# Layer 3 attention of a four-layer decoder: score blocks in cycles of three instead of two

## The reference

```python
def _L3_attn_ref(x, proj_w, proj_b, wq, wk):
    ...
    proj = jnp.einsum('bsd,ed->bse', x, proj_w) + proj_b
    flat = jnp.transpose(proj.reshape(B, S, H, hd), (2, 0, 1, 3)).reshape(H, B * S, hd)
    q = jnp.einsum('hnd,hde->hne', flat, wq)
    k = jnp.einsum('hnd,hde->hne', flat, wk)
    logits = jnp.einsum('hne,hme->hnm', q, k) / jnp.sqrt(jnp.asarray(D, x.dtype))
    attn = jax.nn.softmax(logits, axis=-1)
    out = jnp.einsum('hnm,hmd->hnd', attn, flat)
    ...
x = x + _L3_attn_ref(_layernorm(x, axis=-1), L3_attn_proj_w, L3_attn_proj_b, L3_attn_wq, L3_attn_wk)
```

## Time and profile before

| | us |
|---|---|
| median of 3 runs | 3333.8 (3326.77 to 3339.62) |
| span of the profiled execution | 3397.0 |
| probes and scores run, in that span | 2430 to 3142 |
| PE busy, whole span | 3009.1 (89%) |
| DVE busy | 2235.3 (66%) |
| ACT busy | 1822.0 (54%) |
| POOL busy | 1132.7 (33%) |

### The profile page before, as it was taken

One profiled execution on the slowest core, in us unless ns is written; L12 is line 12 of the kernel. 1 busy time (PEld: TensorE's weight loads), 2 busy tenths in 40 slices (PEclk: granted clock), 3 DMA queues, 4 the chain that ended last, 5 costly groups with the idle time before them and its releaser, 6 DMA issues. The chain is left out here.

```text
span 3397.0 us, 59298 instructions
## 1 busy us (share of the span) xinstructions
PE 3009.1 (89%) x20925; PEld 1857.6 (55%) x20929; DVE 2235.3 (66%) x4489; ACT 1822.0 (54%) x4182; POOL 1132.7 (33%) x1288
## 2 busy tenths in 40 slices
PE   7979759998887799987799989797799999999889
PEld 4656548877664556653467657454333333333567
DVE  6777645454546656667567747525589999996672
ACT  6967713333213344445566645211278888888554
POOL 3535555433432022215166653012111111221333
PEclk9999869999998999998889999898789999999989
DMA  9300156665530000022000032132401111110300
GB/s 301 133 9 2 47 203 210 207 188 173 158 101 26 26 1 1 1 73 85 33 1 1 1 118 106 64 109 88 113 1 20 20 21 20 21 20 1 125 13 25
DMA packets 158228, 243.61 MB, mean 72 GB/s; under 512 B 21298, under 2 KB 130482, under 8 KB 152482
## 3 DMA queue, kind: packets, MB, share of 16 engines
q1 hardware_dynamic: 144114, 202.05, 19.6%
q0 software_dynamic: 13824, 37.77, 3.4%
HBM read 132.64 MB, written 107.10 MB: 71 GB/s over the span
## 5 line engine op out<-in xcount | busy, mean ns | idle before, releaser
L4783 DVE TENSOR_REDUCE peaks<-ps 128x2 f32<-128x1024 f32 x512 | 617.6, 1219 | 64.8 <-PE ps L4727 63.0
L4820 ACT ACTIVATE attn<-ps 128x512 f32<-128x512 f32 x1024 | 558.8, 596 | 113.1 <-PE ps L4717 56.8
L4717 PE MATMUL ps<-queries,keys 50*128 50x512 f32 x1024 | 383.8, 455 | 0.0
L4727 PE MATMUL ps<-keys,queries 50*128 50x512 f32 x1024 | 370.2, 468 | 12.8 <-DVE peaks L4783 7.9
L4742 PE MATMUL ps<-attn,head_values 128*32 128x256 f32 x4096 | 332.3, 397 | 9.2 <-ACT output L4831 9.2
L4717 PEld LDWEIGHTS ps<-queries,keys 50*128 50x128 f32 x1024 | 157.6, 188 | 215.6 <-ACT attn L4820 197.5
L1239 POOL TENSOR_TENSOR attn_w<-attn_w,attn_share 128x512 f32<-128x512 f32 x128 | 131.7, 1050 | 373.0 <-DVE attn_share L1085 373.0
L2133 PE MATMUL ps<-experts,tileT 128*128 x884 | 232.0, 385 | 2.1 <-issue 2.1
L2340 DVE COPY normed<-ps 128x256 f32<-128x256 f32 x221 | 93.8, 424 | 202.9 <-PE ps L2149 106.8
L4742 PEld LDWEIGHTS ps<-attn,head_values 128*32 128x32 f32 x4096 | 82.3, 108 | 197.9 <-issue 108.6
L2194 ACT ACTIVATE tileT<-ps 128x256 f32<-128x256 f32 x221 | 84.6, 383 | 168.4 <-PE ps L2117 115.7
(11 more groups left out here) (733 smaller groups left out, 7164.5 us busy)
## 6 DMA issues: line engine op xcount, KB each, us to landing
tile_in<-routed_rows SPq DMA_DIRECT2D x244, 128.0 KB, 2.2
expert_rows<-normed SPq DMA_DIRECT2D x221, 128.0 KB
routed_rows<-zeros SPq DMA_DIRECT2D x2, 8064.0 KB, 48.1
experts<-in_L_ffn_experts SPq DMA_DIRECT2D x4, 3072.0 KB
routed_rows<-zeros SPq DMA_DIRECT2D x1, 12160.0 KB, 67.0
kT<-L_xattn_keys SPq DMA_DIRECT2D x8, 1024.0 KB
v<-L_xattn_values SPq DMA_DIRECT2D x8, 1024.0 KB, 8.7
experts<-in_L_ffn_experts SPq DMA_DIRECT2D x8, 1024.0 KB
```

What stands on the lines that cost most here:

```text
L4717: nc.tensor.matmul(bank(("score", n)), keys[pair % 2][rows, sl(kt)], queries[pair % 2][rows, sl(c, CHUNK)], start=True, stop=True).then_in ...
L4727: last = nc.tensor.matmul(k.ps[:, SB + p % PB, :], queries[pair % 2][rows, sl(t)], keys[pair % 2][rows, sl(c, CHUNK)], start=True, stop=True)
L4783: v.tensor_reduce(peaks[:, r % 2, i // CHUNKS, :, i % CHUNKS], k.ps[:, at:at + 2, :], AX.X, ALU.max).then_inc(s["maxed"], 1)
L4820: nc.scalar.activation(attn[:, n % RING, :], bank(("score", n)), ACT.Exp, scale=1.0 / 16.0).then_inc(s["read"], 1)
```

## The change

The loop on PE goes in cycles of three score blocks. With n0 the first of the three, a cycle does: probe n0 + 49, score n0, score n0 + 1, probe n0 + 50, probe n0 + 51, score n0 + 2 (one probe, number 0, is done ahead of the loop). These six alternate between the halves of the array. Then come, as a rule, three quarters of a mixing, 128 columns each: a unit has 32 quarters, spread over its 10 or 11 cycles, with 2 to 4 in a cycle. A call of `mix` takes the quarters of one mixing, so a cycle that passes from one mixing to the next has two calls. `unturn` stands at the end of a cycle, `out` and `take` on ACT follow the same cycles, and the places of POOL's and DVE's small steps move by 2 or 3 blocks (`SUM` from 17 to 20, `DIVIDE` from 24 to 26). The banks (4 for probes, 3 for scores) and the ring of 16 stay as they were, and so does every instruction of DVE's reductions and ACT's exponentials.

```diff
+        CYCLE, QUARTER, MIX_BEHIND = 3, CHUNK // 4, 8
         steps = range(-LEAD, TOTAL + SPAN)
-        OUT, UNTURN, SUM, DIVIDE, TURN, RAISE = 6, 15, 17, 24, 5, 8
+        UNTURN, SUM, DIVIDE, TURN, RAISE = 15, 20, 26, 5, 8
...
+        quarters_in, ended_in = {}, {}
+        for u_ in range(UNITS):
+            at = u_ * SPAN + MIX_BEHIND
+            cycles = range(at + -at % CYCLE, at + SPAN, CYCLE)
+            for i, n_ in enumerate(cycles):
+                quarters_in[n_] = range(u_ * SPAN + i * SPAN // len(cycles), u_ * SPAN + (i + 1) * SPAN // len(cycles))
+            ended_in[cycles[-1]] = u_
...
-                def mix(m, half):
+                def mix(m, first, last_one):
                     u, part = m // 8, m % 8
-                    columns = sl(half, CHUNK // 2)
+                    columns = slice(first * QUARTER, (last_one + 1) * QUARTER)
...
-                for n in steps:
-                    if n < 16 - LEAD and n % 4 == 0:
-                        value(4 + (n + LEAD) // 4)
-                    if n % 2 == 0:
-                        for p in (n + LEAD, n + LEAD + 1):
-                            if p < TOTAL:
-                                probe(p)
-                        if scored(n):
+                probe(0)
+                for n0 in steps[::CYCLE]:
+                    for n in range(n0, n0 + CYCLE):
+                        if n < 16 - LEAD and n % 4 == 0:
+                            value(4 + (n + LEAD) // 4)
+                    for n in range(n0, n0 + CYCLE):
+                        p = n + LEAD + 1
+                        if n == n0 + 1 and scored(n):
                             score(n)
-                        if scored(4 * (n // 4 - 2)):
-                            mix(n // 4 - 2, n % 4 // 2)
-                        if scored(n + 1):
-                            score(n + 1)
-                    if ended_at(n, UNTURN) is not None:
-                        unturn(ended_at(n, UNTURN))
+                        if p < TOTAL:
+                            probe(p)
+                        if n != n0 + 1 and scored(n):
+                            score(n)
+                    quarters = quarters_in.get(n0, ())
+                    for m in sorted({q // 4 for q in quarters}):
+                        here = [q % 4 for q in quarters if q // 4 == m]
+                        mix(m, here[0], here[-1])
+                    if unturned_at(n0 + CYCLE - 1) is not None:
+                        unturn(unturned_at(n0 + CYCLE - 1))
...
-                    if ended_at(n, OUT) is not None:
-                        out(ended_at(n, OUT))
-                    if ended_at(n, UNTURN) is not None:
-                        take(ended_at(n, UNTURN))
+                    if n - CYCLE + 1 in ended_in:
+                        out(ended_in[n - CYCLE + 1])
+                    if unturned_at(n) is not None:
+                        take(unturned_at(n))
```

More of the change, by code:

```diff
@@ L4647, in l3_attn @@
         mixed_bank = k.ps[:, 7, :]
+        CYCLE, QUARTER, MIX_BEHIND = 3, CHUNK // 4, 8
         steps = range(-LEAD, TOTAL + SPAN)
-        OUT, UNTURN, SUM, DIVIDE, TURN, RAISE = 6, 15, 17, 24, 5, 8
+        assert LEAD % CYCLE == 0 and len(steps) % CYCLE == 0
+        UNTURN, SUM, DIVIDE, TURN, RAISE = 15, 20, 26, 5, 8
         def scored(n):
@@ L4660, in ended_at, with unturned_at @@
             return u if n % SPAN == i and 0 <= u < UNITS else None
+        def unturned_at(n):
+            found = [ended_at(n - i, UNTURN) for i in range(CYCLE)] if n % CYCLE == CYCLE - 1 else []
+            return next((u for u in found if u is not None), None)
+        quarters_in, ended_in = {}, {}
[5 more added lines that the diff above has]
+            ended_in[cycles[-1]] = u_
         slot_of = {}
@@ L4664, in l3_attn @@
             jobs = [("score", n_)] if scored(n_) else []
-            if ended_at(n_, UNTURN) is not None:
-                jobs.append(("unturn", ended_at(n_, UNTURN)))
+            if unturned_at(n_) is not None:
+                jobs.append(("unturn", unturned_at(n_)))
             for job in jobs:
@@ L4730, in probe @@
                         last.then_inc(s["probed"], 1)
-                def mix(m, half):
+                def mix(m, first, last_one):
                     u, part = m // 8, m % 8
-                    columns = sl(half, CHUNK // 2)
-                    if half == 0:
+                    columns = slice(first * QUARTER, (last_one + 1) * QUARTER)
+                    if first == 0:
                         pe.wait_ge(s["read"], slot_of["score", 4 * m + 3] + 1)
-                    if part == 0 and half == 0:
+                    if part == 0 and first == 0:
                         pe.wait_ge(s["fetched"], u // CHUNKS + 1)
@@ L4742, in mix @@
                         last = nc.tensor.matmul(mixed_bank[sl(strip, PAD), columns], head_values[:, u // CHUNKS % 2, strip % 2, 2 * part + strip // 2, :],
-                                                attn[:, (4 * m + strip) % RING, columns], start=part == 0 and half == 0, stop=part == 7 and half == 1,
-                                                skip_group_check=True)
-                    if half == 1:
+                                                attn[:, (4 * m + strip) % RING, columns], start=part == 0 and first == 0,
+                                                stop=part == 7 and last_one == 3, skip_group_check=True)
+                    if last_one == 3:
                         last.then_inc(s["mixed"], 1)
```

## The result

The changed kernel takes 3388.6 us (median of 4 runs, 3382.3 to 3397.6), the one before, run beside it, 3336.3 us (3326.8 to 3339.6). The ratio is 1.0171, with a 95% interval from 1.0148 to 1.0194: 52 us slower. Forecast were 3382 us and 48 us slower.

What follows compares the result with a forecast made beforehand. PE was taken as the bound before, a PE-DVE loop through the probe banks after. 29.6 units at 1.6 us more (49 unrounded), less 2 at the low clock, added 48 to 3333.8: 3382 us, range 3345 to 3425.

Steps and rivals of the forecast that it cites:

- PE set the pace before: Runs and half mixings on PE take 1.233 us per two score blocks; DVE's reductions follow at 1.13.
- PE's work falls to 1.67 a cycle: Run of six 0.89 plus mixing 0.78 gives 1.67 us for three blocks, where 1.85 were.
- The loop: Waiting probe, mixing, partner probe and reductions: 3.02 + 1.13 = 4.15 us for three pairs, 1.385 a pair against 1.233.
- What a unit has once: Transposes add 0.35 us and DVE's small steps 0.23 to the loop's share; a unit takes 22.7 us, 1.6 more.
- The copy to `output`: The mixing's wait for `outed`, 0.36 us per unit, goes, since the next mixing comes a whole run of 0.89 later.
- The number of units and the low clock: 474 pairs are 29.6 units, 49 us more unrounded; 14 pairs at the low clock save 2 us.
- second calls of `mix`: Four added weight loads in half of the cycles, up to 0.03 us each time, +5 us at most, taken as nothing.
- probes alone, DVE's pace in both: First 24 pairs of the stage run at DVE's pace before and after, so no difference was counted.
- Signs named ahead: Reduction spacing 1.13, 1.13, 1.9; DVE idle 100 to 140 us; PE's probe waits 80 to 130; unit 22.4 to 23.2.
- Rival 1: Probe wait costs nothing and shorter PE work pays out: unit about 19.1 us, kernel 3275 us; chance 0.10.
- Rival 2: Clock falls as the loop leaves PE idle about 0.8 us of every 4.15: some 3480 us; chance 0.06.
- Rival 3: Waiting PE pulls probe weight loads ahead, 0.22 off the loop: unit 21.5 us, kernel 3345 us; chance 0.04.

Runs made afterwards that it cites:

- Half reductions: Row-max reduction reading 256 instead of 512 columns per bank, in three kernels: the one before 3330.3 us, changed 3275.3 us, whole pairs 3313.2 us.
- whole pairs: Changed kernel with four probes in even cycles and two in odd, so no probe pair is split by a mixing: 3324.3 us, ratio to before 0.9965.
- dosed: Changed kernel with quarters dealt unevenly: short mixing (about two quarters) between a pair's probes 3360.6 us, long mixing (about four) 3422.8 us.
- put alone into the old kernel: Kernel before with probes moved on by one, so a half mixing splits every probe pair: 3475.1 us, ratio 1.0408; control with pairs unsplit 3334.5 us.
- second traces: Kernels rerun unchanged for another trace, one run each: the one before 3341.6 us, changed 3385.2 us, whole pairs 3336.2 us.

## Why the prediction was right, step by step

**PE set the pace before: right.** Half reductions left the unit at 21.09.

**PE's work falls to 1.67 a cycle: right.** Run 0.89 and mixing 0.78 stand in the whole pairs' trace; in the changed kernel the mixing is 0.78 too.

**The loop: right, term by term.** From the load of the waiting probe to the mixing 0.43, the mixing 0.78, from the partner's load to its reduction 0.54, each as reckoned. The sum with the reduction's length, the 0.05 to the load and the spacing of 1.13 was 4.15, and 4.16 for three pairs was measured. Three experiments show it as cause: taken away (whole pairs, -64 us), dosed (-28 and +34), and put alone into the old kernel (+138, of which 123 by the longer unit).

**What a unit has once: right.** 22.7 was forecast, 22.8 measured. Of that 16 / 3 x 4.16 = 22.2 is the loop, so the small steps take 0.6, as said. The copy to `output` fell off the path as forecast.

**The number of units and the low clock.** 29.6 x 1.7 = 50, less 2, is 48, and from first to last score the second traces differ by 48.8. That it fits to 1 us is partly luck: the spell at 0.50 was taken as the same in both kernels, and in these traces it lasted 19 us after the first score before and some 12 in the changed one. The second calls of `mix`, bounded by 5 us and taken at nothing, were not measured apart; the unit leaves 0.1 us, 3 us in all, for them and for rounding. One term was wrongly put at nothing: "probes alone, DVE's pace in both". The first pairs alternate with value projections, the changed kernel splits them as well, and it takes 5.0 us longer to its first score. With it the sum is 53, where the medians differ by 52.

**Signs named ahead.** Spacing 1.14, 1.13, 1.89 (said: 1.13, 1.13, 1.9), idle before the reductions 131 (said: 100 to 140), a unit of 22.8 (22.4 to 23.2), the wait for `output` gone. One was set too high: PE's probes wait 74.6 us for `peaks`, not 80 to 130. The forecast took waits from start to start, and the record of the matmul before reaches into each of them.

**The rivals.** Rival 1, shorter PE work paid out, needs the loop gone. Half reductions do that (with half of the keys left out), whole pairs do it in part, since they cost PE a slot. That half reductions land on the 3275 us of this rival is luck in part, since their unit is 19.3 and not 19.1. Rival 2, the clock, stayed away: 1.00 from 2550 to 3050 with a gap of 0.47 us in PE's own records once per loop. The swing that the Trainium skill describes in "TensorE: Matmul & The Clock Gate", "A second HAM failure mode: psum-queue depth-cycling", does not show at such gaps. Rival 3, loads pulled ahead of a waiting run, did not happen: 0.62 of idle time on the load side stands before probe 13 (2708.53), and its first matmul has its load exposed as before.

## What to carry to other kernels

When a consumer frees buffers in pairs, keep the pair's two producers together in the producer's program: whatever in-order work stands between them becomes part of the buffers' turnaround, and the freed engine time cannot be used. Before making an engine's order denser, write down the path from "buffer free" to "consumer starts again" and compare it with the time the other buffers cover, here 1.9 us against 1.13. Where the path is the longer one, moving work out from between the two or making the consumer faster pays at once, as the runs here show; making the producer's work shorter elsewhere should not. The start of a stage needs a look of its own: here the same split cost 5 us there with the new order and 15 in the old kernel.

## What the runs showed of the hardware

The spell at the granted clock of 0.50, the lower of its two levels (1.2 GHz), at the start of this stage ended at quite different times under the same instructions: 20 and 48 us after the first score for the whole pairs, with PE's records 85% and 92% busy over the spell; 32 and 19 us after it for the kernel before. By the prediction's estimates such a spell costs a kernel that PE bounds more (2.16 us for two blocks against 1.233) than the changed one (2.02 against 1.385); no run measured that apart. I had taken its length as fixed.
